# Moving the edge-attribute scatters of a four-block graph network: 32 into the first convolution's sums, 50 more into the second's

## The reference, cut to what matters

```python
x = _layernorm(x + _L0_gnn_ref(...))   # 2 gated layers
x = _layernorm(x + _L1_gnn_ref(...))   # 3 relational layers
x = _layernorm(x + _L2_gnn_ref(...))   # GCN
x = _layernorm(x + _L3_gnn_ref(x, edge_index, edge_attr_16, ...))
# in _L3_gnn_ref:
rec_attr = _scatter_mean(edge_attr, row, N)     # by sender
sent_attr = _scatter_mean(edge_attr, col, N)    # by target
```

## Time and profile before

| | |
|---|---|
| median of 3 runs | 2637.78 us (2634.90 to 2644.64) |
| profiled execution, first to last instruction (its span) | 2969.2 us |
| its own time beside the span | no other figure was taken; the span stands for it |
| PE busy | 2492.2 us (84%) |
| PEld busy | 2211.7 us (74%) |
| VectorE busy | 1808.3 us (61%) |
| ScalarE busy | 868.5 us (29%) |
| GpSimd busy | 1585.9 us (53%) |
| mean granted TensorE clock | 0.913 |
| attribute scatters, SBUF part `w` | 352, 353.2 us busy |
| attribute scatters, SBUF part `rec` | 64, 67.4 us busy |

### The profile page before, as it was taken

One profiled execution on the slowest core, in us unless ns is written; L12 is line 12 of the kernel. 1 busy time (PEld: TensorE's weight loads), 2 busy tenths in 40 slices (PEclk: granted clock), 3 DMA queues, 4 the chain that ended last, 5 costly groups with the idle time before them and its releaser, 6 DMA issues.

```text
span 2969.2 us, 45704 instructions
## 1 busy us (share of the span) xinstructions
PE 2492.2 (84%) x15625; PEld 2211.7 (74%) x15625; DVE 1808.3 (61%) x6126; ACT 868.5 (29%) x1546; POOL 1585.9 (53%) x1706
## 2 busy tenths in 40 slices
PE   7587878888687899746999998998989897878798
PEld 3366666666387889436999997888988886777797
DVE  4565656575576777423876655676865554433585
ACT  2355555554354111213222231111311110443102
POOL 0656666663577666542566626666456665565200
PEclk9789888888799999857999999999999999898899
DMA  7312112110398666106888887877788774565793
GB/s 273 111 50 53 51 51 53 51 52 25 103 281 260 166 173 170 38 27 210 274 272 270 269 266 231 240 228 211 238 273 251 226 234 134 174 213 198 232 267 105
DMA packets 271515, 520.11 MB, mean 175 GB/s; under 512 B 61999, under 2 KB 115554, under 8 KB 270501
## 3 DMA queue, kind: packets, MB, share of 16 engines
q1 hardware_dynamic: 185053, 289.49, 31.2%
q0 software_dynamic: 86224, 227.59, 26.6%
HBM read 323.93 MB, written 192.99 MB: 174 GB/s over the span
## 4 chain that ended last, share of the span: by engine, by line
PE 69%; issue 10%; DMA 7%; DVE 6%; another core or an unknown queue 4%; ACT 2%; POOL 2%; SPq 0%; DVEq 0%; POOLq 0%; ACTq 0%
PE ps L1058 21%; PE ps L1030 10%; PE ps L892 7%; PE ps L1043 6%; PE ps L1245 5%; PE ps L1289 4%; PE ps L886 4%; PE ps L878 4%; DMA chunks<-xs 2%; DMA rec<-chunks,idx 2%; DMA srow<-lanes_of_slots 1%; DVE shot L2033 1%; POOL attributes L744 1%; PE ps L1112 1%
## 5 line engine op out<-in xcount | busy, mean ns | idle before, releaser
L735 POOL DMA_INDIRECT rec<-chunks,idx x596 | 588.5, 987 | 500.5 <-PE ps L1058 184.9
L1058 PE MATMUL ps<-dhot,rec 128*128 128x168 f32 x4768 | 757.2, 312 | 70.4 <-issue 35.3
L1058 PEld LDWEIGHTS ps<-dhot,rec 128*128 128x128 f32 x4768 | 703.8, 194 | 99.6 <-issue 77.6
L2054 DVE TENSOR_SCALAR dhot<-iota,dcode 128x168 f32<-128x168 f32 x2384 | 584.6, 311 | 216.7 <-remote 102.4
L1030 PE MATMUL ps<-hrow,shot 126*128 126x128 f32 x4000 | 516.3, 284 | 63.8 <-issue 29.5
L735 POOL DMA_INDIRECT msg<-messages,idx_buf x416 | 398.2, 957 | 307.3 <-issue 189.7
L1030 PEld LDWEIGHTS ps<-hrow,shot 126*128 126x128 f32 x4000 | 493.7, 199 | 81.7 <-issue 65.9
L1386 ACT ACTIVATE xs<-ps 128x512 f32<-128x512 f32 x500 | 295.1, 597 | 763.5 <-PE ps L1030 393.8
L744 POOL DMA_INDIRECT attributes<-w,rank_to x352 | 353.2, 1004 | 213.1 <-issue 102.2
L2033 DVE TENSOR_SCALAR shot<-srow,lane_no 126x512 f32<-126x512 uint8 x500 | 230.2, 486 | 117.4 <-PE ps L1030 51.2
L892 PE MATMUL ps<-big,lane1h 128*128 128x300 f32 x832 | 231.6, 432 | 9.3 <-issue 8.0
(11 more groups left out here) (304 smaller groups left out, 2538.6 us busy)
## 6 DMA issues: line engine op xcount, KB each, us to landing
chunks<-xs SPq DMA_DIRECT2D x375, 256.0 KB
tmp<-inverse_counts SPq DMA_DIRECT2D x36, 1008.0 KB
chunks<-xs SPq DMA_DIRECT2D x125, 258.0 KB
srow<-lanes_of_slots SPq DMA_DIRECT2D x100, 320.0 KB
grec<-chunks SPq DMA_DIRECT2D x125, 256.0 KB
messages<-big SPq DMA_DIRECT2D x25, 504.0 KB
trow<-lanes_of_targets SPq DMA_DIRECT2D x30, 320.0 KB
rec<-chunks,idx POOLq DMA_INDIRECT x596
```

What stands on the lines that cost most here:

```text
L735: eng.indirect_dma_start(buf, None, table, bass.IndirectOffsetOnAxis(ap=index, axis=0)).then_inc(sem, 16)
L1058: last = mm(ps[:, 4 + i % 2, (v % 3) * WT:(v % 3 + 1) * WT], rec[:, v % RS, j * P:(j + 1) * P], dhot[:, v % DS, j * WT:(j + 1) * WT], star ...
L2054: last = vec.tensor_scalar(dhot[:, v % DS, j * WT:(j + 1) * WT], iota[:, 0:WT], dcode[:, v, j:j + 1], None, ALU.is_equal)
```

## The change

The 32 scatters at the head of set 1 leave the first gated cell and go into the sums of k = 1, one behind every fourth gather (windows 3, 7, ... 127). GpSimd then waits only for the 80 others before it lets gathers write over `rec`, from which the later ones read. Of set 2, 30 instead of 80 go in a row, and they now wait for the first tile of k = 2 to be copied, where before they waited only for their data. The other 98 instead of 48 go behind two of every three gathers of k = 2, from window 1 on. Sets 3 and 4 keep their places.

```diff
-AT_FIRST = {1: 32, 2: 80, 3: 40, 4: 40}
+AT_FIRST = {1: 32, 2: 30}
...
-                if n == 0:
+                if n == (AT_FIRST[1] if k == 1 else 0):
                     eng.wait_ge(q("attr_loaded"), 16 * {1: 2, 2: 3, 3: 5, 4: 6}[k])
...
-            for n in range(AT_FIRST[1]):
-                send_attrs(1, n)
...
-            attrs_sent(eng, 1)
+            eng.wait_ge(q("attr_sent"), 16 * (G * len(AT[1]) - AT_FIRST[1]))
...
                 if k == 2:
-                    for n in range(AT_FIRST[k]):
-                        send_attrs(k, n)
+                    after(eng, "x1_evac", 2, 1)
+                    for n in range(AT_FIRST[2]):
+                        send_attrs(2, n)
...
-                    if k == 2 and v % 3 == 1 and AT_FIRST[k] + v // 3 < G * len(AT[k]):
-                        send_attrs(k, AT_FIRST[k] + v // 3)
-                    n = 2 * (v // 3 - 4) + v % 3 - 1
-                    if k >= 3 and v % 3 > 0 and 0 <= n < G * len(AT[k]):
+                    if k == 1 and v % 4 == 3 and v // 4 < AT_FIRST[1]:
+                        send_attrs(1, v // 4)
+                    n = 2 * (v // 3) + v % 3 - 1 + (AT_FIRST[2] if k == 2 else -8)
+                    if k >= 2 and v % 3 > 0 and 0 <= n < G * len(AT[k]):
                         send_attrs(k, n)
```

## The result

The change makes the kernel slower, by about 1%: 2668.44 us in the median of 4 runs (2657.92 to 2670.13) against 2638.81 us (2634.90 to 2644.64) for the kernel before, a ratio of 1.0096 with a 95% interval of 1.0076 to 1.0117. By the ratio that is 25 us, 20 to 31. The time is 22 us above the predicted figure of 2646 us, above the forecast's own range (2634 to 2654 us) and close to what rival 1 gave (2666 us). It lies at the upper end of the whole range, 2606 to 2668 us: the ratio applied to the 2637.78 us that the prediction started from gives 2663 us, inside it, while the median, 2668.44 us, is at the bound.

The account below looks back on a forecast made before the run. It took DMA to bound the tiles and saw PE busy 224.9 of 239.2 us in the sums of k = 1. Unrecorded terms 0 + 0 + 0.5 + 0 + 5 + 3 = +8.5 us on 2637.8 gave 2646 us, range 2606 to 2668 us.

Parts of the forecast that it names:

- rival 1: Sums of k = 1 and k = 2: GpSimd becomes the bound, +28 us, 2666 us; chance 0.31.
- The waits of 59.7 us: Second gated cell and norm: three recorded waits without known releaser, 59.7 us together, taken as absent in an unrecorded run.
- Unrecorded, if the waits aren't there, 0: the 80 are covered.: Second cell and norm: removing 80 scatters gains 0 us unrecorded, at most 59.7 us recorded.
- Rivals 2 and 3: Second cell's waits are the kernel's own: won, -42 us, 2596 us, chance 0.19; or given back, 2622 to 2637 us, 0.12.
- if it stays at 145 us the scatters weren't the cause: Sign, sums of k = 1 to first tile of k = 2: without scatters, 145.1 us should shrink to about 85 us.
- The 331 us must have gone somewhere: Whole kernel: reason for choosing the unrecorded sum, the recorded span being 331 us above the median of 2637.78 us.
- 32 scatters leave the first gated cell: First gated cell: removing these scatters gains 0 us unrecorded, at most 6.2 us.
- 30 scatters behind the first tile's copy: First tiles of k = 2: the row ends about when the first gather starts, +0.5 us; another 0 unrecorded, 8 us recorded.
- 32 scatters in the sums of k = 1: Sums of k = 1: four late scatters, +5 us, with bounds of 0 and 41 us; the least trusted term.
- if the sums of k = 1 lengthen by over 15 us: Sums of k = 1: a sign that the prediction is wrong; it expected 240 to 250 us there.
- 50 more scatters in the sums of k = 2: Sums of k = 2: +3 us unrecorded, 37 us recorded; in turns 1 to 3, bounds of 1 and 36.7 us.
- the case that I preferred: Whole kernel: waits not there unrecorded and GpSimd's queue just fits, 2638 to 2651 us; chance 0.38.

Follow-up runs that it names:

- e0: The kernel before, unchanged, recorded again for a second profile: 2648.39 us, span 2646.6 us.
- e11: The kernel before with the 32 scatters of set 1 never sent, set 2 as before: ratio 1.0013 (0.9995 to 1.0031).
- e2: The kernel before with only set 2 moved as in the change, set 1 left beside the first cell: ratio 1.0027 (1.0016 to 1.0039).
- e3: The kernel before with only set 2 moved, its 30 not waiting for the first tile's copy: ratio 1.0017 (1.0002 to 1.0032).
- e1: The kernel before with only set 1's 32 scatters moved, behind every fourth gather of k = 1: ratio 1.0094 (1.0077 to 1.0111).
- e4: The kernel before with only set 1's 32 scatters moved, in threes behind gathers v % 12 = 10 of k = 1: ratio 1.0060 (1.0047 to 1.0073).
- e9: The kernel before with only set 1's 32 scatters moved, behind gathers v % 12 = 5, 7, 9 of k = 1: ratio 1.0069 (1.0048 to 1.0091).
- e10: The change with set 1's 32 scatters behind gathers v % 12 = 5, 7, 9 instead: ratio to the kernel before 1.0078 (1.0055 to 1.0101).
- e7: The kernel before, scatters unmoved, plus 32 awaited GpSimd copies of 128 x 516 behind every fourth gather of k = 1: ratio 1.0048 (1.0034 to 1.0063).
- e6: The kernel before with set 1's 32 scatters each issued twice, behind every second gather of k = 1: ratio 1.0209 (1.0194 to 1.0223).

## Why the prediction was right and where it was wrong

**The waits of 59.7 us are not the kernel's: right.** "Unrecorded, if the waits aren't there, 0: the 80 are covered." They are: 75.9 us for cell and norm without them, 76.6 us with them. Rivals 2 and 3, which rest on real waits, fall. But the test that I named for it was a poor one: "if it stays at 145 us the scatters weren't the cause". The stretch did shrink to 75.9 us with the clock at 0.84 above 0.66, and it is as short, at 0.82, in e0, where the scatters still stand there. Only the kernel before, recorded again, could tell.

**"The 331 us must have gone somewhere", into the recorder: wrong.** The recorded execution of the kernel after is the fastest of its four, and e0 (2648.39 us) lies among the other executions of its kernel (2630.05 to 2648.88 us). The Trainium skill's "NOTIFIC — the notification-queue block", section 10, says that writing a record costs an engine no cycle; section 7.1 has, in one of its three modes, a full queue stall the producer of the records. Twelve profiles of the experiments and that of the change show no such stall. Whether a record costs nothing is shown by no run here: the record gives a span and a clock for each of the four executions of the change and for each execution of the experiments, so none of these is known to have run without a recorder. I had taken one odd execution for what a recorder does in each. The term, 0 for the 80 scatters, is right; the reason that I chose it for is not, and that part is luck.

**"32 scatters leave the first gated cell", 0: right** (e11, at most 1.3 us).

**"30 scatters behind the first tile's copy", +0.5 us: right as far as it can be read.** The row ends at 1191.25 and the first gather starts at 1191.56, within the 2 us that I named, 40.1 us behind the first tile's copy against 39.6 us in e0. e2 less e3 is 3 us by the ratios, with intervals that overlap; their traces show no difference between the last gather of k = 1 and the first of k = 2 (130.1 and 130.3 us).

**"32 scatters in the sums of k = 1", +5 us: the step that failed.** It measures +25 us alone (e1), five times as much, of which the traces show 17 to 20 us in the sums (240.8 us against 220.5 to 224.2 us in the kernels without them); the rest is within the interval of the ratio. I worked out room: "three scatters to twelve gathers" need 1.57 us per window and "the stretch gives 239.2 / 149 = 1.61 us". Two things are wrong in it. The stretch holds the landing of the first record and the last windows, in which GpSimd issues nothing. The row of the gather gave the better figure: 967.7 to 1195.7 us is 228 / 148 = 1.54 us, and 1.49 to 1.51 us in the undisturbed kernels; fifteen instructions of 1.27 us need 1.59 us per window. There was no room. And I spread GpSimd's waits out evenly, "1.24 us every 3.5 gathers". For the disturbed execution that was not far off; it is not what the kernel does otherwise. In e0 16 of the 34 waits for PE are only the 0.30 us between two instructions, most of the slack is one wait of 3 us in twelve gathers, and two of three scatters fall where they delay the loop that ends in it. The text also set a bound for itself, "if the sums of k = 1 lengthen by over 15 us": from first to last gather they are 14.6 us longer than in e0 and 16.6 to 18.3 us longer than in e2, e3 and e11, so by most of what there is to compare with that sign of being wrong came.

**"50 more scatters in the sums of k = 2", +3 us: right** (+4 us in e3, some 5 us in the traces). The queue was "as long as the turns", and longer: turns 1 to 3 with 178 instructions take 234.3 us after and 226.0 us in e0, and 236.1 and 234.2 us in layers 3 and 4, the same density, the same length. The upper bound of 36.7 us, from 271.0 and 264.0 us, came from the disturbed execution.

**The sum.** 0 + 0 + 0.5 + 0 + 5 + 3 was forecast. Set 1 and set 2 measure 25 + 7 = 32 us alone (e1, e2) and 25 us (20 to 31) together. The result lies in the range because the range covers rival 1; the case that I preferred, 2638 to 2651 us, missed. Rival 1, "GpSimd becomes the bound of the sums", is nearest to what happened, and its price of 28 us fits; of its two halves, "half of the 32 scatters late, 20 us" was nearer than my four. Its mechanism is half of it: GpSimd's queue as a whole, 19.1 us for twelve gathers and three scatters, is the bound in e4, e9 and e10, while in the change the loop is, with 19.9 us. Its ground against, that layers 3 and 4 carry the same density, says nothing about k = 1: there windows follow each other every 1.5 us without tiles between them, in layers 2 to 4 every 322 / 148 = 2.2 us.

## What to carry to other kernels

Work that an engine does in a queue is free only where that queue has room over its own gathers: take first and last start of the instruction and divide by their number, not the length of a stretch with its start and tail. Then look where the slack lies; if it is one wait in a fixed period, find the loop that ends in it, and ask of each place whether it is in the loop or beside it. A stand-in for a cost, like the copies of e7, is read only after asking what else it slows. And where a profile's span and the measured time are 12% apart, record the kernel again before any term is priced from it.

## What the runs showed of the hardware

One profiled execution of fourteen has a span of 2969.2 us and 59.7 us of waits that no instruction explains; in each of the others the span is some 2 us below its time. An indirect DMA of GpSimd, a gather of 128 x 516 or a scatter of 128 rows of 64 bytes, occupies its queue for 1.27 us in the mean of the change's sums (175.50 us busy in 181, and 0.30 us ahead of each), and 213 of them set the length of the sums of e6, 275 us. A scatter in the row beside the first gated cell takes 1.34 us (e0). A gather lands 3.5 to 3.7 us after its issue in the median of these sums (the change, e2, e6), up to 4.86 us in the chain of e0, about three of its own issue times; with one gather per buffer in a ring of six this latency, and not only throughput, is part of the period. Beside a GpSimd copy of 128 x 516 in fp32, four `dhot` of VectorE took 1.86 us in place of 0.96 us (e7).
